# Gated cross-attention block: q of the first four batches in one piece, and later homes for the small loads and the q stores

## The reference, cut to what matters

```
xn  = layernorm(x)
Q   = xn @ Wq.T + bq;  K = ctx @ Wk.T + bk;  V = ctx @ Wv.T + bv      # 16 heads of 16
O   = softmax(Q K.T / 4) V                                           # per batch and head
x1  = x + tanh(g_xattn) * (O @ Wh.T + bh)
out = x1 + tanh(g_ffn) * moe(layernorm(x1))                          # top 2 of 8 low-rank experts
```

## Time and profile before

| | us |
|---|---|
| median of 3 runs | 552.71 (552.25 to 553.4) |
| the profiled execution | 549.46 |
| its span | 547.6 |
| what lies around the span | 1.86 |
| PE busy | 511.1 (93%) |
| DVE, ACT, POOL busy | 358.8 (66%), 258.7 (47%), 293.0 (54%) |
| mean granted PE clock | 0.978 of full speed |

### The profile page before, as it was taken

How to read it: one execution, slowest core, us unless ns; L and a number is a source line. 1 busy time by engine, 2 the same in 40 slices (tenths; PEclk the granted TensorE clock), 3 DMA queues, 4 the chain that set the end, 5 groups by cost and what they waited for, 6 DMA issues and landing times.

```text
span 547.6 us, 11814 instructions
## 1 busy us (share of the span) xinstructions
PE 511.1 (93%) x4366; PEld 466.0 (85%) x4366; DVE 358.8 (66%) x779; ACT 258.7 (47%) x579; POOL 293.0 (54%) x339
## 2 busy tenths in 40 slices
PE   3669799999998999999998999999999999999994
PEld 3536788988887888888787999999999999999993
DVE  7664567777776777888765876865466654755443
ACT  2334655555555555555767533353334443433331
POOL 7625055666665444744368983763357443853441
PEclk9978899999999999999999989999999999999998
DMA  7627455678767776765411000001000000000000
GB/s 215 183 83 198 162 134 141 145 185 187 176 158 151 161 172 157 182 145 124 107 21 16 9 1 1 2 0 31 2 1 1 30 1 1 1 1 31 0 1 30
DMA packets 50888, 45.83 MB, mean 84 GB/s; under 512 B 33967, under 2 KB 40275, under 8 KB 50832
## 3 DMA queue, kind: packets, MB, share of 16 engines
q1 hardware_dynamic: 41502, 22.56, 17.5%
q0 software_dynamic: 6704, 15.93, 12.3%
q10 hardware_dynamic: 2626, 6.59, 4.0%
HBM read 20.59 MB, written 6.66 MB: 50 GB/s over the span
## 4 chain that ended last, share of the span: by engine, by line
PE 81%; DVE 6%; DMA 6%; ACT 3%; issue 1%; SPq 1%; POOL 1%; POOLq 0%; DVEq 0%; ACTq 0%
PE bank L1317 12%; PE bank L1181 9%; PE bank L1211 7%; PE bank L1198 7%; PE bank L1369 6%; PE bank L1321 6%; PE bank L1334 6%; PE bank L1158 5%; PE bank L1166 5%; PE bank L1349 4%; DMA QS<-crow 3%; PE bank L1242 2%; PE bank L1352 2%; DVE nmax L922 2%; PE bank L1142 2%; PE bank L1283 2%
## 5 line engine op out<-in xcount | busy, mean ns | idle before, releaser
L922 DVE TENSOR_REDUCE nmax<-bank 100x1 f32<-100x361 f32 x256 | 128.0, 527 | 58.5 <-PE bank L1181 55.3
L407 POOL TENSOR_TENSOR awl<-hb,awh 128x400 fp32r<-128x400 f32 x64 | 71.1, 1113 | 102.4 <-ACT awh L618 102.4
L1181 PE MATMUL bank<-KS,QS 96*100 96x362 f32 x256 | 90.8, 391 | 7.2 <-DVE nmax L922 6.8
L516 ACT ACTIVATE pt<-bank 120x400 f32<-120x400 f32 (+1 forms) x192 | 82.7, 505 | 26.5 <-PE bank L1198 26.5
L618 ACT ACTIVATE awh<-hb 128x400 fp32r<-128x400 f32 x64 | 34.5, 539 | 119.4 <-DVE hb L868 119.2
L861 DVE TENSOR_TENSOR hb<-sil,bank 128x400 f32<-128x400 f32 x64 | 36.5, 570 | 82.9 <-PE bank L1334 38.7
L346 POOL DMA_DIRECT2D KS<-kn x64 | 32.4, 513 | 108.9 <-PE bank L1181 73.4
L1181 PEld LDWEIGHTS bank<-KS,QS 96*100 96x100 f32 x256 | 42.9, 170 | 26.7 <-issue 13.6
L1198 PE MATMUL bank<-QS,KS 97*120 97x200 f32 (+1 forms) x384 | 50.7, 268 | 5.8 <-DMA wh<-whT 3.8
L1198 PEld LDWEIGHTS bank<-QS,KS 97*120 97x120 f32 (+1 forms) x384 | 49.0, 184 | 7.5 <-issue 4.4
L868 DVE TENSOR_TENSOR hb<-hb,wbT 128x400 f32<-128x400 f32 x64 | 47.4, 741 | 2.1
(11 more groups left out here) (182 smaller groups left out, 1134.7 us busy)
## 6 DMA issues: line engine op xcount, KB each, us to landing
KS<-kn SPq DMA_DIRECT2D x128, 90.5 KB, 2.8
KS<-kn POOLq DMA_DIRECT2D x64, 90.5 KB, 2.8
craw<-ctxT POOLq DMA_DIRECT2D x14, 361.0 KB, 5.9
QS<-q_dram POOLq DMA_DIRECT2D x92, 50.0 KB, 4.8
q_dram<-qn SPq DMA_DIRECT2D x6, 400.0 KB, 6.0
o_dram<-on SPq DMA_DIRECT2D x16, 100.0 KB
xr<-o_dram SPq DMA_DIRECT2D x16, 100.0 KB
y<-xs SPq DMA_DIRECT2D x16, 100.0 KB
```

What stands on the lines that cost most here:

```text
L407: nc.gpsimd.tensor_tensor(awl[:, g % 2, slot], hb[:, slot], awh[:, g % 2, slot].bitcast(F32), ALU.subtract).then_inc(m["p_awl"], 1)
L516: nc.scalar.activation(pt[0:TW[t], u % 6, :], pT[u % 3][0:TW[t], 0:CS], ACT.Exp, scale=float(DH) ** -0.5).then_inc(m["act_e"], 1)
L922: nc.vector.tensor_reduce(nmax[:, pos:pos + 1], pS[h % 2][0:S, 0:T], AX.X, ALU.max, negate=True).then_inc(m["dve_s"], 1)
L1181: mm(pS[h % 2][0:S, 0:TP], QS[b % 3][0:96, g, h % 2, j, :], KS[b % 3][0:96, g, j, :], start=True, stop=True).then_inc(m["pe_s"], 1)
```

## The change

- x of batches 2 and 3 is the first load on ACT's queue; x of batches 4 to 7 is loaded ahead of SP's wait for the first context; bks moves from SP's queue to ACT's, behind the first context, and is counted with wk (`wk_in` 32), as bqs is with wq (`wq_in` 32).
- The first q chunk is one piece of four batches. Statistics come in three groups (0 to 3, 4 to 7, 8 to 15) in place of four.
- On DVE the statistics of batches 8 to 15 stand together behind the low part of K of batch 0 and ahead of the first maxima. On ACT the third root stands behind the V copies. `k_proj(0, 0)` waits for both low parts at its start.
- On PE the q projection of chunk 1 stands ahead of the first scores, transposes and projections of chunks 2 and 3 stand earlier, `row_turn(0, 0)` is ahead of `s_head(0, 8)`.
- SP stores chunks 0 and 1 right behind the K copies of batch 0, ahead of the first row of maxima and the K copies of batch 1. ACT stores chunk 2 at the end of step 0 and chunk 3 at the end of step 1.
- bhs, gx, gf and nw are loaded by SP at the end of the prologue, where POOL loaded them at 23 us. The wait for `w_in` (four loads now) leaves PE's prologue for `y_proj(1)`; SP still waits for it ahead of xr. The two tanh move from the end of ACT's prologue to the end of step 0.

Core of the diff:

```diff
             sp.dma_start(wq[:], wqT).then_inc(m["wq_in"], 16)
-            sp.dma_start(bqs[:], bq).then_inc(m["bq_in"], 16)
-            sp.dma_start(bks[:], bk).then_inc(m["bk_in"], 16)
+            sp.dma_start(bqs[:], bq).then_inc(m["wq_in"], 16)
+            x_load(1)
             sp.wait_ge(ctx_in[0], 16)
...
                     for g in range(4):
                         k_stack(0, g)
-                    sp.wait_ge(m["q_l"], 2 * KT)
                     for hl in range(2):
                         sp.dma_start(q_dram[hl, :, 0, KT * S:], qn[:, 0, hl, 1:].rearrange("p b j s -> p (b j s)").bitcast(F32)).then_inc(q_out[0], 16)
                 if i == -1:
+                    sp.wait_ge(m["q_l"], 2 * KT)
+                    for hl in range(2):
+                        sp.dma_start(q_dram[hl, :, 1, :], qn[:, 1, hl].rearrange("p b j s -> p (b j s)").bitcast(F32)).then_inc(q_out[1], 16)
                     sp.wait_ge(m["act_c"], 1)
                     row_store(0, 0)
...
-                    q_store(1)
...
                     sp.dma_start(wh[:], whT).then_inc(m["w_in"], 16)
-                    q_store(2)
-                    sp.wait_ge(m["w_in"], 2 * 16)
+                    sp.dma_start(bhs[:], spread(bh.rearrange("(o d) -> o d", o=1), 0, S)).then_inc(m["w_in"], 16)
+                    sp.dma_start(gx[:], spread(g_x.rearrange("(o d) -> o d", o=1), 0, 128)).then_inc(m["w_in"], 16)
+                    sp.dma_start(gf[:], spread(g_f.rearrange("(o d) -> o d", o=1), 0, 128)).then_inc(m["gf_in"], 16)
+                    sp.dma_start(nw[:], norm_w).then_inc(m["gf_in"], 16)
+                    sp.wait_ge(m["w_in"], 4 * 16)
...
-                if i == 0:
-                    q_store(3)
...
+            act.dma_start(xs[:, 2:4, :], x[2:4].rearrange("b s d -> s b d")).then_inc(x_half, 16)
             act.dma_start(wst[:, 0], wkT).then_inc(m["wk_in"], 16)
             act.dma_start(craw[:, 0, :, 0:T], ctxT[0]).then_inc(ctx_in[0], 16)
-            act.dma_start(xs[:, 2:4, :], x[2:4].rearrange("b s d -> s b d")).then_inc(x_half, 16)
+            act.dma_start(bks[:], bk).then_inc(m["wk_in"], 16)
...
+                if i == 0:
+                    q_store(2)
+                    act.wait_ge(m["w_in"], 4 * 16)
+                    nc.scalar.activation(tgx[:], gx[:], ACT.Tanh).then_inc(m["tg_ok"], 1)
...
+                if i == 1:
+                    q_store(3)
...
             def y_proj(i):
                 wait(pe, "dve_ot", i)
+                if i == 1:
+                    pe.wait_ge(m["w_in"], 4 * 16)
...
-            pe.wait_ge(m["w_in"], 2 * 16)
             pe.wait_ge(m["xnT_ok"], 2 * NC)
-            pe.wait_ge(m["q_l"], KT * NC + KT)
+            pe.wait_ge(m["q_l"], KT * NC)
```

More of the change, by code:

```diff
@@ L225, in _ @@
             sp.dma_start(wq[:], wqT).then_inc(m["wq_in"], 16)
[L226 to L227 removed]
+            sp.dma_start(bqs[:], bq).then_inc(m["wq_in"], 16)
+            x_load(1)
             sp.wait_ge(ctx_in[0], 16)
[L229 to L230 removed]
+            x_load(2)
+            x_load(3)
             sp.wait_ge(m["ones"], 1)
@@ L477, in q_high, with q_store @@
                     act.wait_ge(q_first, 32)
-                nc.scalar.activation(qn[:, c % 2, 0, r, j, :], pT[j][:, r.start * S:r.stop * S].rearrange("p (b s) -> p b s", b=r.stop - r.start),
-                                     ACT.Identity, bias=bqs[:, j:j + 1]).then_inc(m["q_h"], 1)
+                nc.scalar.activation(qn[:, c % 2, 0, :, j, :], pT[j][:, 0:CS].rearrange("p (b s) -> p b s", b=4), ACT.Identity, bias=bqs[:, j:j + 1]).then_inc(m["q_h"], 1)
+            def q_store(c):
+                act.wait_ge(m["q_l"], c * KT + KT)
+                for hl in range(2):
+                    act.dma_start(q_dram[hl, :, c, :], qn[:, c % 2, hl].rearrange("p b j s -> p (b j s)").bitcast(F32)).then_inc(q_out[c % 2], 16)
             def k_high(b, j):
@@ L558, in _ @@
             row_out(0, 0)
-            turned(4)
-            turned(5)
             normed(3)
+            q_high(2, 0)
             v_out(1, 0)
+            q_high(2, 1)
             v_out(1, 1)
-            q_high(2, 0)
-            v_out(1, 2)
-            q_high(2, 1)
             turned(6)
             turned(7)
+            v_out(1, 2)
             q_high(3, 0)
             q_high(3, 1)
-            act.wait_ge(m["sm_in"], 4 * 16)
-            nc.scalar.activation(tgx[:], gx[:], ACT.Tanh).then_inc(m["tg_ok"], 1)
-            nc.scalar.activation(tgf[:], gf[:], ACT.Tanh).then_inc(m["tgf_ok"], 1)
             def w_high(p):
@@ L736, in ctx_high, with stat @@
                 nc.vector.tensor_copy(cth[:, b % 2, 0], craw[:, b % 2]).then_inc(m["ctx_h"], 1)
-            def stat(b0, b1):
-                dve.wait_ge(x_in[b0 // 4], 16)
-                for b in range(b0, b1):
+            def stat(c):
+                dve.wait_ge(x_in[c], 16)
+                for b in range(4 * c, 4 * c + 4):
                     if b == 2:
@@ L1132, in turn, with q_proj @@
                 last.then_inc(m["xnT_t"], 1)
-            def q_proj(c, j, p=0):
-                lo, hi = (0, CS) if c else ((0, S), (S, CS))[p]
+            def q_proj(c, j):
                 if j == 0:
-                    pe.wait_ge(m["wq_in"], 16)
-                    pe.wait_ge(m["xnT_ok"], 2 * c + 2 if c or p else 1)
-                if c:
-                    pe.wait_ge(m["q_l"], 2 * c + j + 1)
+                    pe.wait_ge(m["wq_in"], 32)
+                    pe.wait_ge(m["xnT_ok"], 2 * c + 2)
+                wait(pe, "q_l", (c - 1) * KT + j + 1)
                 for k in range(KT):
-                    last = mm(pT[j][:, lo:hi], wq[:, k, j * 128:(j + 1) * 128], xnT[:, k, c * CS + lo:c * CS + hi],
+                    last = mm(pT[j][:, 0:CS], wq[:, k, j * 128:(j + 1) * 128], xnT[:, k, c * CS:(c + 1) * CS],
                               start=k == 0, stop=k == KT - 1)
@@ L1393, in _ @@
             k_proj(0, 1)
-            turn(1)
-            q_proj(0, 0, 1)
-            q_proj(0, 1, 1)
+            turn(2)
+            turn(3)
             pe.wait_ge(m["wkv_l"], 2)
@@ L1402, in _ @@
             v_proj(0, 2)
-            turn(2)
-            turn(3)
+            q_proj(1, 0)
+            q_proj(1, 1)
             s_head(0, 0)
@@ L1407, in _ @@
             s_head(0, 2)
-            q_proj(1, 0)
             s_head(0, 3)
-            q_proj(1, 1)
+            turn(4)
+            turn(5)
             s_head(0, 4)
@@ L1427, in _ @@
             s_head(0, 10)
+            q_proj(2, 1)
             s_head(0, 11)
@@ L1431, in _ @@
             s_head(0, 12)
-            q_proj(2, 0)
+            turn(6)
+            turn(7)
             s_head(0, 13)
```

130 lines of the change are left out of this document (49 added, 81 removed).

## The result

| | before | changed |
|---|---|---|
| median of four executions each | 552.48 us (548.82 to 553.4) | 540.76 us (535.67 to 547.62) |
| ratio, with its 95% interval | | 0.9718 (0.9641 to 0.9795) |
| the profiled execution, its span | 549.46, 547.6 | 535.67, 533.9 |
| mean granted clock in it | 0.978 | 0.990 |
| start of step 0 | 57.86 | 45.85 |

Ratios leave out executions that ran slower at a lower granted clock: here two of the four of the changed kernel (544.72 and 547.62), and over all series 2 of its 16 and 1 of 51 of the kernel before, which leaves medians of 538.3 and 550.2 us, 12.0 us gained (11.1 with them in), where the prediction has 10.7 to the median.

A forecast was written before the change was run, and what follows sets the result against it. PE was taken to bound the main loop, with prologue losses standing in full. From 549.46, 10.4 us for an earlier step 0 and 1.0 for clock, plus 0.5 for ACT, gave 538.6; with 3.25 to the median, 542 us, range 538 to 550.

The forecast's parts named there:

- third part: From row_turn to PE's last q projection: 12.7 us; 11 at full clock, 15 with half clock all through.
- fixed 3.25 us: Whole kernel: the median of the runs lies 3.25 us above the profiled execution, added to reach the forecast median.
- second part: From first score to first row of maxima: DVE sets the pace, 7 us; ends 4.8 and 10; gain 7.6.
- from there to step 0: After PE's last q projection: the last chunk's q_high and q_low hold step 0 for 1.3 us.
- First part: Prologue up to the first score: possible at 26.5 us, losing 1.3 us to before.
- collision of DVE with POOL: Prologue: DVE and POOL can block each other; two collisions in the first part would cost 2.5 us.
- Step 0: Steps 0 and 1: clock saves 1.0 us, ACT's added transfers and tanh cost 0.5 us together.
- 1 (the half clock stays): Prologue projections still run at half clock, step 0 starts at 51 instead of 47.5: 545.5 us, chance 0.13.
- 2 (the queue on SP): A w_in load needs 12 us, the row comes 4 us late, PE stands in step 0: 547.5 us, chance 0.10.
- 3: No change: the prologue's first score hangs on the four-batch q store, released at 27: 552 us, chance 0.06.
- 4: Slower: rows of maxima come late in eleven late steps, each waiting 1.7 us: 557.5 us, chance 0.09.
- The signs: After: first score 25 to 28, step 0 45 to 50; wrong if step 0 after 52 or row wait over 3.

The follow-up runs named there:

- e4: Changed kernel with the last statistics, their root on ACT and the dependent projections and transposes in their old places; ratio to before 0.9984, 549.26 us.
- e5: The changed kernel unaltered, timed again against the kernel before in six executions; 540.45 us, ratio 0.9833.
- e12: The changed kernel unaltered, timed a third time in six executions; 537.88 us, ratio to before 0.9794.
- e7: Changed kernel with DVE's small addition (variance plus epsilon) removed: ACT takes the root with eps as bias, DVE the reciprocal; 540.51 us, ratio to before 0.9848.
- e1: Kernel before with one edit: PE waits for wh at y_proj(1), not ahead of step 0; 547.88 us, ratio 0.9954.
- e2: As e1, and SP stores q chunk 1 ahead of the first row of maxima and batch 1's K copies; 545.77 us, ratio to before 0.9894.
- e9: Changed kernel with the six small loads at the prologue's end issued by POOL at about 26 us instead of SP; 537.72 us, ratio to before 0.9788.
- e11: As e10, with the first chunk's q projection cut into batch 0 and batches 1 to 3; 536.78 us, ratio to before 0.9771.
- e10: Changed kernel with the edits of e9 and e7 together; 539.51 us, ratio to before 0.9808.

## Where the prediction held, and the step that failed

**What bounds, and the direction: right.** The start of step 0 was the number that mattered. It came 12.0 us earlier (10.4 predicted), and the span became 13.7 us shorter, 1.7 of them behind that start.

**The step that failed is the third part of the sum**, from the first row of maxima to the end of PE's last q projection. It was put at 12.7 us: the 13.0 of the kernel before, "part of it at half clock", and only 0.3 off. It took 10.2 us in all three profiles of the changed kernel, PE busy all through and at full clock. The time by stretch (columns as above), first of the kernel before, then of the changed one, then of e4:

```profile
41.15:54.11 12.96, 12.44 (x58) 9.44 (x56) 5.44 (x12) 6.25 (x14) 7.65 (x12) 0.83 0.81 206
34.10:44.29 10.19, 10.19 (x51) 7.02 (x51) 6.27 (x13) 5.81 (x13) 9.14 (x15) 1.00 0.77 186
40.51:53.91 13.40, 12.99 (x59) 9.06 (x59) 6.28 (x13) 7.05 (x15) 7.51 (x12) 0.83 0.66 158
```

So the half clock of before went with the gaps that the change closes, and came back with them in e4. The prediction's own end for this part, 11 us at full clock, was the true case, and was not the one put into the sum; with the measured 10.2 us the sum for the profiled execution is 536.1 us. The second step that failed is the fixed 3.25 us from the profiled execution to a median. Term by term:

| term | predicted | first profile | e5 | e12 |
|---|---|---|---|---|
| first score | 26.5 | 25.47 | 25.97 | 24.92 |
| second part, to the row | 7 | 8.6 | 7.2 | 8.6 |
| third part, to the last q projection's end | 12.7 | 10.2 | 10.2 | 10.2 |
| from there to step 0 | 1.3 | 1.6 | 1.6 | 1.6 |
| step 0 to the end | 489.2 | 488.05 | 494.7 | 490.75 |
| around the span | 1.86 | 1.77 | 1.8 | 1.85 |
| the profiled execution | 538.6 | 535.67 | 541.54 | 537.85 |

- First part: the way was right row for row (normalized x at 7.39, bks landed at 9.3, q projection from 10.87 at the slow pace, K copy as the last releaser). The store was mis-sized: 3.5 us taken, 2.35 measured (17.35 to 19.70). The projection was 0.75 us shorter than put in this profile; in e5 it took 5.67 us.
- Second part: the collision of DVE with POOL that the prediction named and left out of the sum was there, 2.47 us. But it is not the main cause of the 1.6 us: e5 has it too (1.79 us), at a clock of 1.00, and needs 7.2 us. In the first profile and in e12 the clock over this part was 0.80. A stretch of half clock that the sum did not have costs 1.4 us there. In e7, where most of the collision is gone, the part takes 6.3 us.
- Luck: the second part came out too long and the third too short, so of errors of 2.5 and 1.6 us 1.65 are left at the start of step 0.
- Step 0: counted as 1.0 less 0.5 for ACT. Its own length fell from 14.42 to 13.47 us. ACT's new transfers and tanh cost nothing: it lasts 12.9 us in e1 and e2, which lack them, and in e4, e9 and e11, which have them. Where it lasted 14.4 us (before, e10, e12) its first products ran at half clock. Behind it PE waited less for rows: 3.7 us in sum to 320 us, where it was 5.0.
- The fixed 3.25 us was no constant. It was the difference of one profile from three runs; over 51 executions the kernel before has a median of 550.2, 2.5 us under the 552.71 it was reckoned from. The time of an execution goes, in the main, with its mean granted clock. Of the executions of the kernel before that stood beside the experiments, those at 0.978 took 547.5 to 549.0 us and those at 0.972 took 549.6 to 553.7; those at 0.975 overlap both, 547.9 to 552.4. It does not explain all: the changed kernel took from 539.85 to 544.72 us at 0.984. Its profiles stood at 535.67, 541.54 and 537.85 beside medians of 540.76, 540.45 and 537.88.
- "A measurement of this kernel can tell about 0.2%": the intervals here are 0.3% to 0.8% to either side.

**The parts.** By step 0: moving the wait for wh 1.65 us (e1); all edits but the order of the statistics 2.4 (e4); that order 9.6. Of these 9.6, 6.9 stand in the second part, where the prediction put 7.6, and 3.2 in the third, which takes e4 13.4 us; the first score of e4 is 0.5 us earlier.

**The rivals.** 1 (the half clock stays): false here for the third part, true in e4. In the second part a stretch of it stayed in two of three profiles, and the argument against it, no gap over 2 us, does not hold: gaps of 1.34 and 1.39 us stood ahead of it in the first profile. 2 (the queue on SP): its mechanism is true in e5, with half clock behind it; its time, 547.5, came in none of the three medians. "This fits with about 1 us to spare: nothing" was wrong by 0.3 us in the first profile and 3.0 in e5. It rested on 5.9 us for a small load, where g_x took 6.17 to 9.25, and on six issues by 44.5, where the last was issued at 46.96: one tiny load alone held SP's queue for 2.31 us. 3 and 4: no sign; the waits for rows after step 0 became shorter.

**The signs.** Those for the first profile came as written, but for the row, 0.29 us late. In e5 two signs of a wrong forecast are there: PE waits 3.03 us for the row, and step 0 to the end is 5.0 us longer than 489.7.

The prediction lets the 8.2 us of wh beside stores of the same SP queue stand for the interleaving of several engines' transfers. That row has one engine only; e10 and e9 show two.

Left open: why g_x lands after 6.2 us in one execution and after 9.3 in another; why the same 1.55 us gap ahead of step 0 is followed by half clock in e10 and e12 and by full clock in the first profile, e2, e4 and e11; and where the stretches at half clock between 250 and 300 us come from; nothing in the diff touches them.
